# Relative value products in two column tiles of half an octet's queries, with the second expert matrix six steps behind the first

## What is computed

```python
rel_idx = jnp.arange(L)[:, None] - jnp.arange(L)[None, :] + (L - 1)
rpe = rel_emb[:, rel_idx]                 # 32 x L x L
rpe_v = rpe[hf:]                          # 16 x L x L, a table of its own for each pair i, j
...
attn = jax.nn.softmax(logits, axis=3).astype(jnp.float32)
wv  = jnp.einsum('bhij,bhdj->bhdi', attn, v)
wve = jnp.einsum('bhij,dij->bhdi', attn, rpe_v)
out = (wv + wve)
...
for i in range(K):                        # K = 2, the two best gates of a row
    h = jax.nn.gelu(jnp.einsum('btd,edf->ebtf', x * top_p[..., i:i+1], W1) + b1)
    out = out + jnp.einsum('ebtf,efd->btd', h, W2) + b2_sum
```

## Time and profile before

| what | value |
|---|---|
| median of 3 runs | 2934.63 us (2927.7 to 2934.8) |
| the profiled execution | 2932.71 us, span 2930.8 us |
| mean granted TensorE clock | 0.994 |
| TensorE matmul / weight load busy | 2862.8 / 2294.8 us |
| VectorE / ScalarE / GpSimd busy | 1975.8 / 1957.8 / 1025.8 us |

### The profile page before, as it was taken

The page is one execution under the profiler, slowest core; times in us unless marked ns, Lnnn a source line. Parts: engine busy times, 40 slices in busy tenths (PEclk is TensorE's granted clock), DMA queues, the critical chain, the costliest instruction groups (busy, mean ns, idle before and its releaser), DMA issues.

```text
span 2930.8 us, 65392 instructions
## 1 busy us (share of the span) xinstructions
PE 2862.8 (98%) x21348; PEld 2294.8 (78%) x21348; DVE 1975.8 (67%) x4885; ACT 1957.8 (67%) x4640; POOL 1025.8 (35%) x999
## 2 busy tenths in 40 slices
PE   6998899999999999999999999999999999999998
PEld 6996777777777778777777777777777787777776
DVE  4665666776676667666666666666766676666665
ACT  4564467776766667766666677766666677666666
POOL 0000233434333434434333334444333344343334
PEclk9999999999999999999999999999999999999999
DMA  9994011111111011111110111111110111111100
GB/s 184 213 207 137 17 31 36 31 36 36 34 33 32 15 36 31 36 36 36 31 36 19 28 36 31 36 36 36 31 34 13 36 31 36 36 36 31 33 9 12
DMA packets 104390, 134.79 MB, mean 46 GB/s; under 512 B 10110, under 2 KB 98750, under 8 KB 99902
## 3 DMA queue, kind: packets, MB, share of 16 engines
q1 hardware_dynamic: 97442, 131.00, 19.8%
q10 hardware_dynamic: 6896, 3.09, 0.5%
HBM read 118.97 MB, written 15.07 MB: 46 GB/s over the span
## 4 chain that ended last, share of the span: by engine, by line
PE 83%; ACT 7%; DVE 4%; issue 3%; DMA 2%; SPq 1%; POOL 0%; DVEq 0%; ACTq 0%; POOLq 0%
PE bank L398 20%; PE bank L407 7%; PE bank L499 6%; PE bank L553 6%; PE bank L552 6%; PE bank L520 6%; PE bank L408 6%; PE bank L411 6%; PE bank L585 4%; ACT arena L949 4%; PE bank L506 4%; PE bank L534 3%; PE bank L562 2%; DVE mx L745 1%; SPq L339 1%
## 5 line engine op out<-in xcount | busy, mean ns | idle before, releaser
L1014 POOL TENSOR_TENSOR arena<-arena 128x386 f32<-128x386 f32 x672 | 734.5, 1100 | 710.4 <-ACT arena L893 702.5
L892 ACT ACTIVATE arena<-bank,b_s 128x386 f32<-128x386 f32 x1024 | 596.0, 582 | 445.5 <-DVE arena L614 396.0
L398 PE MATMUL bank<-arena,w_s 128*128 128x386 f32 x2048 | 831.2, 490 | 0.3 <-POOL arena L1014 0.2
L614 DVE TENSOR_TENSOR arena<-bank,ratio 128x386 f32<-128x386 f32 x1024 | 571.2, 559 | 269.0 <-PE bank L411 247.4
L893 ACT ACTIVATE arena<-arena,b_s 128x386 f32<-128x386 f32 x1024 | 623.2, 609 | 0.0
L407 PE MATMUL bank<-x_hi,w_hi 128*128 128x386 f32 x1024 | 577.2, 564 | 2.5 <-ACT x_hi L965 1.8
L949 ACT ACTIVATE arena<-bank,mx 128x193 f32<-128x193 f32 x800 | 325.9, 425 | 163.9 <-DVE mx L745 163.9
L398 PEld LDWEIGHTS bank<-arena,w_s 128*128 128x128 f32 x2048 | 369.1, 190 | 20.9 <-POOL arena L1014 10.6
L408 PE MATMUL bank<-x_hi,w_lo 128*128 128x386 f32 x1024 | 350.2, 342 | 0.0
L411 PE MATMUL bank<-x_lo,w_hi 128*128 128x386 f32 x1024 | 348.8, 341 | 0.0
L499 PE MATMUL bank<-rw,arena 128*128 128x193 f32 x1600 | 318.5, 339 | 4.1 <-DVE arena L735 3.9
(11 more groups left out here) (155 smaller groups left out, 4215.1 us busy)
## 6 DMA issues: line engine op xcount, KB each, us to landing
a_rep<-u_scratch SPq DMA_DIRECT2D x32, 1600.0 KB, 9.8
arena<-in_x SPq DMA_DIRECT2D x192, 196.0 KB
g_bc<-g_scratch SPq DMA_DIRECT2D x64, 193.0 KB, 3.6
hk<-in_txt SPq DMA_DIRECT2D x32, 128.0 KB, 2.5
u_scratch<-k_f SPq DMA_DIRECT2D x32, 100.0 KB, 2.2
u_scratch<-q_f SPq DMA_DIRECT2D x32, 100.0 KB, 2.2
out<-o_s SPq DMA_DIRECT2D x64, 48.5 KB
out<-o_s SPq DMA_DIRECT2D x64, 48.0 KB
```

The costliest lines, as they stand in the source:

```text
L398: mm(yb[:, 0:T2], w2_s[:, f, :], gelu1[:, f % RING, :], start=(f == 0), stop=(f == NF - 1)).then_inc(S["w2_done"], 1)
L614: v.tensor_tensor(gelu2[:, f % RING, :], zb[f % 2][:, 0:T2], ratio[:, :], ALU.mult).then_inc(S["z2_done"], 1)
L892: a(gelu1[:, f % RING, :], zb[f % 2][:, 0:T2], ACT.Gelu, bias=b1_s[:, f:f + 1]).then_inc(S["g_done"], 1)
L1014: g.tensor_tensor(gelu1[:, f % RING, :], gelu1[:, f % RING, :], gelu2[:, f % RING, :], ALU.add).then_inc(S["pool_sum"], 1)
```

## The change

Each matmul of `rel` becomes two, one for queries 0 to 3 of the octet and one for queries 4 to 7: 64 columns of `rv` as weights, 16 x 4 columns of weights as moving operand, written to partitions 0 to 63 or 64 to 127 of the bank through column tile 0 or 64. An octet takes 64 columns of the bank instead of 128, and VectorE's mask operation reads each of them twice, by a broadcast axis. LAG goes from 4 to 6, and the list of steps is another one. In it the steps `~a` stay 4, `~w2t` are 6 instead of 4, `c` 16 instead of 17, `C` 12 instead of 11. (Lines from 556 on are two higher in the changed kernel.)

```diff
-LAG = 4
+LAG = 6
...
-    "qs0 ~grow ~w2t vt ~w2t am0 log0 am1 ~w2t qs1 log1 ~w2t qs2 am2 log2 qs3 log3 ~ot am3 log4 log5 ~hres ~bcast log6 log7 qs4 ~xin hkeep log8 log9 log10 ~otr log11 log12 txt tr0 ~a st1 tr1 ~a rel0 ~a tr2 rel1 nb1 tr3 inv rel2 tr4 rel3 tr5 rel4 ~ocopy tr6 xt1 rel5 ~a c rel6 proj pv0 rec0 gmean c pv1 rec1 gvar place0 place1 C gaff c omean c c C C nqk ovar C c C C oaff onorm C oh2 c swap mean2 C var2 nv top C c gate C C c c c c c c c gate2 c c"
+    "~w2t am0 vt ~grow ~w2t ~w2t log0 qs0 ~w2t am1 ~w2t qs1 log1 am2 ~w2t log2 ~ot log3 log4 log5 qs2 am3 log6 log7 ~hres qs3 ~bcast ~xin hkeep qs4 ~otr log8 log9 log10 log11 txt log12 tr0 ~a st1 tr1 ~a rel0 ~a tr2 ~a nb1 rel1 tr3 c ~ocopy c rel2 tr4 c inv rel3 tr5 xt1 rel4 tr6 rel5 rel6 proj pv0 gmean c rec0 gvar pv1 rec1 place0 place1 C gaff C omean c c C C ovar nqk C C C oaff onorm c c oh2 C C swap mean2 c c var2 C top c c C c gate c c C nv gate2 c c"
...
-                        part = pv[g % 2][:, (o - octs[0]) * P:(o - octs[0] + 1) * P]
-                        mm(part, rv[:, (8 * o + P) * HD:(8 * o + P) * HD + P], pr[0][:, o, :, :], start=True, stop=False)
-                        m = mm(part, rv[0:JC[1][1], 8 * o * HD:8 * o * HD + P], pr[1][0:JC[1][1], o, :, :],
-                               start=False, stop=True)
+                        for c, (j0, jn) in enumerate(JC):
+                            w = (8 * o + (0 if c else P)) * HD
+                            for half in range(2):
+                                m = mm(pv[g % 2][64 * half:64 * half + 64, (o - octs[0]) * 64:(o - octs[0]) * 64 + 64],
+                                       rv[0:jn, w + 64 * half:w + 64 * half + 64], pr[c][0:jn, o, :, 4 * half:4 * half + 4],
+                                       start=(c == 0), stop=(c == 1), skip_group_check=True, tile_position=(0, 64 * half))
...
-                    v.tensor_tensor(wm[:, g * GRP:g * GRP + w, :, :],
-                                    pv[g % 2][:, 0:w * P].rearrange("p (o b r) -> p o b r", o=w, r=8),
-                                    K["mask_r"].unsqueeze(1).unsqueeze(1).broadcast_to([P, w, BH, 8]),
+                    v.tensor_tensor(wm[:, g * GRP:g * GRP + w, :, :].rearrange("p o b (h r) -> p o b h r", h=2),
+                                    pv[g % 2][:, 0:w * 64].rearrange("p (o b r) -> p o b r", o=w, r=4).unsqueeze(3).broadcast_to([P, w, BH, 2, 4]),
+                                    K["mask_r"].rearrange("p (h r) -> p h r", h=2).unsqueeze(1).unsqueeze(1).broadcast_to([P, w, BH, 2, 4]),
```

More of the change, by code:

```diff
@@ L90 @@
 SCHEDULE = (
-    "qs0 ~grow ~w2t vt ~w2t am0 log0 am1 ~w2t qs1 log1 ~w2t qs2 am2 log2 qs3 log3 ~ot am3 log4 log5 ~hres ~bcast log6 log7 qs4 ~xin hkeep log8 log9 log10 ~otr log11 log12 txt tr0 ~a st1 tr1 ~a rel0 ~a tr2 rel1 nb1 tr3 inv rel2 tr4 rel3 tr5 rel4 ~ocopy tr6 xt1 rel5 ~a c rel6 proj pv0 rec0 gmean c pv1 rec1 gvar place0 place1 C gaff c omean c c C C nqk ovar C c C C oaff onorm C oh2 c swap mean2 C var2 nv top C c gate C C c c c c c c c gate2 c c"
+    "~w2t am0 vt ~grow ~w2t ~w2t log0 qs0 ~w2t am1 ~w2t qs1 log1 am2 ~w2t log2 ~ot log3 log4 log5 qs2 am3 log6 log7 ~hres qs3 ~bcast ~xin hkeep qs4 ~otr log8 log9 log10 log11 txt log12 tr0 ~a st1 tr1 ~a rel0 ~a tr2 ~a nb1 rel1 tr3 c ~ocopy c rel2 tr4 c inv rel3 tr5 xt1 rel4 tr6 rel5 rel6 proj pv0 gmean c rec0 gvar pv1 rec1 place0 place1 C gaff C omean c C C ovar nqk C C C oaff onorm c c oh2 C C swap mean2 c c var2 C top c c C c gate c c C nv gate2 c c"
 ).split()
```

## The result

The changed kernel takes 2803.58 us in the median of 3 runs (2803.53 to 2807.42) against 2934.63: a ratio of 0.9565, interval 0.9541 to 0.959. That is 131.0 us, or 4.1 us in each of 32 turns. Its profiled execution took 2807.42 us with a span of 2805.0 at a mean clock of 0.993.

A forecast was written before the change was run, and what follows sets the result against it. TensorE, busy 98% of the span, sets a turn's time. Products save 5.34 us, round trips cost 1.7, the order gives 0.4: 4.04 a turn, 129 over 32 turns, from 2932.7 to 2804 us; ends 2765 and 2833.

The forecast's parts named there:

- The round of two tiles: In `rel`, one record for each column tile side by side takes 0.058 us, between 0.055 and 0.063.
- The products save: In `rel`, 100 rounds take 5.8 us instead of 11.14, saving 5.34 us a turn (4.8 to 5.6).
- rival A: In `rel`, weights are not loaded beside products in column tiles: a round takes 0.113 us, 2980 us in all; chance 0.06.
- Rival B: In `rel`, TensorE can't be fed four instructions in 0.058 us: a round takes 0.094, 2919 us in all; chance 0.08.
- The round trip: Switching TensorE from whole array into tiles and back around `rel` costs 0.34 us, five times a turn: 1.7 (1.2 to 1.7).
- The order: The new list gives back half of TensorE's 0.84 us of waits at lines 426, 432 and the logits' end: 0.4 us.
- signs of being wrong: A round near 0.11 or 0.094 us, TensorE idle before line 520 for copies, or W1 steps awaiting gelus in the transposing stage.
- The later W2 steps cost nothing by themselves: In the experts' steps, a later W2 step only finds its sum made earlier, and gelus stay covered: costed at nothing.
- The mask: VectorE's mask operation on `rel`'s output, reading half the bank twice, still takes 0.69 us a group: costed at nothing.
- rival C: In the transposing stage, VectorE's copies hold up the next transposes, losing 2.5 of 4.0 us a turn: 2853 us; chance 0.15.

The follow-up runs named there:

- e4: The changed kernel with both halves in column tile 0, leaving out the relative values of queries 4 to 7 of each octet: 2987.52 us.
- e6: The changed kernel with four column tiles of 32 columns in all groups instead of two of 64: 2875.05 us.
- e1: The kernel before with the products in two column tiles, keeping the old list of steps and LAG 4: 2838.88 us.
- e11: The changed kernel with `rel4` moved behind `tr6` to `rel5` and `rel6`, and one step `c` moved behind `xt1`: 2797.78 us.
- e2: The kernel before with the new list of steps and LAG 6, keeping the old products 128 wide: 2924.29 us.
- e7: e1 with LAG 6 and two more `~w2t` steps in the old list: 2831.66 us.
- e3: The changed kernel with LAG 4 and without two of its `~w2t` steps: 2914.69 us.
- e12: e11 with four column tiles of 32 columns in group 0 alone: 2976.78 us.
- e5: The changed kernel with the loop over halves outside the one over key blocks, four records per tile in turn: 2813.63 us.

## Why the prediction was right

**The total.** Forecast 2804 us, measured 2803.6. The sum was 4.04 us a turn, the runs show 4.1.

**The round of two tiles** was taken from two neighbours as 0.058 us. It is 0.058, and e4 shows that it is the tiles' work side by side: in one tile the records of a round go one after another. (0.085 / 97 is 0.00088 and not 0.00085 a column, 0.056 for 64; the slip changes nothing.) The products save 11.14 - 5.84 = 5.3 us a turn, as predicted. This falls with rival A. The rule of the Trainium skill (TensorE: Matmul & The Clock Gate, "The mechanism") that loads overlap with running products only when their row group differs does not hold here: both tiles span all rows, and a load and a product of 64 columns each, for both tiles, fit into 0.058 us, where rival A's load and product one after another needed 0.113. Even in one tile (e4) a record with its load takes 0.0625. The same section also names a background weight buffer into which a load can go ahead; the rows do not speak against that, and no run here tells whether it is the way. Rival B falls too: four instructions in 0.058 us, and in e6 eight in (0.70 - 0.15) / 16 = 0.034, are fed without a gap inside a group.

**The round trip** was the most uncertain term, five times 0.34 from the logits. A finer reading of starts gives 0.09 going in, 0.05 in the first round, 0.09 coming out and 0.06 in the first transposes, 0.29 in all. By the rows: 1.08 us less 16 x 0.058 leaves 0.15, and the eight transposes that follow directly take 0.85 (1511.00 to 1511.85) instead of 0.79, and 0.10 lie ahead of the group (1509.64 to 1509.92 is 0.28, of which a W1 record takes 0.18): 0.31. Five are 1.5, not 1.7: a mis-sizing of 0.2 that stayed within the range. e1, with six of them, fits the same size: 5.3 - 6 x 0.31 - 0.3 for the copy wait is 3.1 a turn, and 101.0 / 32 is 3.16. e11, with four, does not: its turns are 0.12 us shorter and not 0.29; why was not found.

**The order** was put at 0.4 by halving three waits of 0.84. e2 measures 0.42 to 0.49 on the old products by its medians and ratio; its loop turns are only 0.28 shorter (82.72 for 83.00). But it is not a half of each: the waits at 426 and 432 went wholly (0.28 and 0.23, together 0.51), and the one at the end of the logits did not shrink but got 0.33 longer (10.7 us over 32 turns). These three leave 0.18; the rest was gained at places that were not located. The number was about right, its make-up was not. And under the tiles the order gives more, 35 us, because it spares a sixth round trip and a wait for a copy. The prediction charged five trips and no copy wait in the same sum, so this was counted, though under other names. Of its signs of being wrong one came, in another place: W1 steps do wait for gelus now, in the experts' stretch and not in the transposing stage, 0.2 us a turn. It comes with the order and not with the tiles: e2 has it too (7.0 us, 32 times), e1 has not (1.0 us, twice).

**"The later W2 steps cost nothing by themselves"** held in e7, but the step of the prediction that treated the lag as indifferent failed: under the new list a lag of 4 costs 3.6 us a turn (e3). The prediction looked at who waits for a late W2 step and not at what a W2 step waits for when it is early, the copy of the last pair's output and GpSimd's last sums, nor at what the two W2 steps among the logits cover, VectorE's mask of their operand. In the change all three are covered, so the total did not suffer.

**The mask** cost nothing, 0.685 us. **The copies** (rival C) do not hold TensorE in the change: VectorE has 15.69 us of work in a stage of 18.94, where 15.4 in 18.8 were forecast, and it is VectorE that waits for the transposes, 14.6 us in all. With the old list a wait for a copy does appear, once a turn, but for ScalarE's, which C did not name.

**What was not seen at all.** The change adds some 50 instructions to TensorE's loop, and the prediction costed none of them, apart from the rate at which they are fed. It came within 16 of a size at which, if the price of e12 holds for it, the kernel would have been slower than before. That nothing was lost was luck, not a step of the argument.

## What to carry to other kernels

Where only a part of a matmul's output is wanted and the parts lie on a diagonal, two column tiles compute half as much in half the time, at some 0.3 us for each round trip from the whole array into tiles and back: group such work, and put other work between tiled groups only where it costs no further trip. Price the instructions of a looped body by their total number too: compare the instruction queue's packets per pass before and after, for here 16 instructions too many cost as much as 80. When a list is written for a lag, test them together; each alone told nearly nothing here.

## What the runs showed of the hardware

- **A longer looped body can be fetched anew in every pass.** With 551 program instructions (1537 issued) no instruction is fetched in a pass; with 567 (1601 issued) nine packets of 16.4 KB come in each pass, which with the gap and the clock costs 6.8 us. The Trainium skill (Advanced Engine Details and Errata, "ISA Cache") gives TensorE 128 KB in lines of 16 KB, 256 instructions each. The packets agree with the line's size, 0.61 MB in 37 of them. The 128 KB do not explain the step by themselves: by the page's figures they hold 2048 instructions, and in e12 a body of 1601 is fetched again.
- **The clock falls after such a gap**: in e12 3.5 us of idle time within 5, and then mostly 6.8 us at the lower level, which about doubles the price; in e6 one gap of 2.3 us, and then 3.4 us at the lower level.
- **TensorE starts matmuls of a free column tile ahead of older ones of a busy tile** (e5, 1.13 us a group against 1.39 in order). The Trainium skill (TensorE: Matmul & The Clock Gate, "The mechanism") has matmuls strictly in order; the rows of e5 disagree for different column tiles.
- **Round lengths of float32 records with loads beside them:** 0.111 us for one of 128 columns, 0.058 for two of 64 side by side, 0.034 for four of 32 side by side.
